# A four-layer graph network on one core: an unused buffer grows from 32 to 64 bytes per partition, and every buffer behind it moves by 32 bytes

## The reference, cut to what matters

```python
def _L0(x, adj, ...):   # 8 heads of 32, pros masked by adj; 4 hops
    q, k, v = x @ Wq.T + bq, x @ Wk.T + bk, x @ Wv.T + bv
    pros = softmax(where(adj == 0, -16384, q k^T))      # per head
    z = v
    for _ in range(4): z = 0.9 * pros @ z + 0.1 * v
    return layernorm(x + z)
def _L1(x, adj, ...):   # one head of 256
    w = softmax(where(adj == 0, -inf, (x @ Wq) (x @ Wk)^T / 16))
    return layernorm(x + (w @ (x @ Wv)) @ Wo + bo)
def _L2(x, adj, ...):   # 8 heads of 32, scaled, masked, output product with Wo
    return layernorm(x + attention(x) @ Wo + bo)
def _L3(adj, x, ...):   # 4 edge labels, mean over each label's neighbours, then a gated update
    weight = (adj == d) / (count + 1e-8)                # d = 1..4
    out = relu(concat_d(weight_d @ x) @ Wd.T + bd)
    r, z = sigmoid(out @ Wri.T + x @ Wrh.T + b), sigmoid(out @ Wzi.T + x @ Wzh.T + b)
    n = tanh(out @ Wni.T + bni + r * (x @ Wnh.T + bnh))
    return layernorm((1 - z) * n + z * x)
```

## The kernel before, in words

| buffers | bytes past a multiple of 64 |
|---|---|
| ident, ident_b, w_hi, w_lo, wo2_sb, row | 0 |
| x_in, xt_in, absent, qT0, kT0, vT0, vnat0, E0, PT0, nmax0, esum0, rsum0 | 0 |
| adj1, no_edge1, xT1, qT1, vnat1, E1, PT1 | 0 |
| absent2, qT2, kT2, vnat2 (and xT2), E2, PT2, nmax2, esum2, rsum2 | 32 |
| adj3, E3, wT, xw (and oT_hi, oT_lo, oT), xT3, rT, zT, nT, out_sb | 32 |
| y0 to y3, xn0, xn1, xT_hi0 to xT_hi3, xT_lo0 to xT_lo3 | 32 |

## Time and profile before

### The profile page before, as it was taken

The page is one execution under the profiler, slowest core; times in us unless marked ns, Lnnn a source line. Parts: engine busy times, 40 slices in busy tenths (PEclk is TensorE's granted clock), DMA queues, the critical chain, the costliest instruction groups (busy, mean ns, idle before and its releaser), DMA issues.

```text
span 1682.3 us, 44431 instructions
## 1 busy us (share of the span) xinstructions
PE 1612.9 (96%) x17552; PEld 1480.5 (88%) x17552; DVE 1131.4 (67%) x2875; ACT 1207.7 (72%) x4008; POOL 782.6 (47%) x774
## 2 busy tenths in 40 slices
PE   4788999999999999999999999999999999999985
PEld 3677999999999999999999999999999999999884
DVE  3566667677766676766667676666767666677642
ACT  4577777777777777777777777877778777777542
POOL 1345444535555454555544455454445554544521
PEclk8999999999999999999999999999999999999997
DMA  5000001110011011001101101111110111100000
GB/s 191 17 23 27 27 27 30 33 33 18 20 33 33 30 33 33 12 26 33 33 30 32 33 5 33 33 30 33 33 33 5 33 33 30 33 27 17 20 7 13
DMA packets 71135, 51.51 MB, mean 31 GB/s; under 512 B 4368, under 2 KB 69904, under 8 KB 70288
## 3 DMA queue, kind: packets, MB, share of 16 engines
q1 hardware_dynamic: 70928, 48.66, 9.4%
HBM read 40.26 MB, written 8.39 MB: 29 GB/s over the span
## 4 chain that ended last, share of the span: by engine, by line
PE 88%; ACT 4%; DVE 3%; issue 3%; POOL 1%; DMA 1%; SPq 0%; POOLq 0%; DVEq 0%; ACTq 0%
PE bank_A L375 14%; PE bank_B L375 10%; PE bank_A L601 6%; PE bank_A L592 5%; PE bank_B L592 5%; PE bank_A L419 5%; PE bank_B L419 4%; PE bank_A L405 4%; PE bank_C L413 3%; PE bank_C L375 3%; PE bank_B L387 3%; PE bank_X L375 3%; PE bank_X L387 2%; PE bank_X L527 2%; PE bank_A L393 2%
## 5 line engine op out<-in xcount | busy, mean ns | idle before, releaser
L797 POOL TENSOR_TENSOR E<-E,rsum 128x512 f32<-128x512 f32 x256 | 276.4, 1085 | 296.7 <-DVE rsum L898 180.3
L805 POOL TENSOR_TENSOR rstd<-var,minus_half 128x2 f32<-128x2 f32 x128 | 90.5, 707 | 216.8 <-DVE var L933 216.8
L375 PE MATMUL bank_A<-xT_hi,w_hi 128*128 128x256 f32 x512 | 137.9, 291 | 14.0 <-DVE xT_lo L868 11.8
L820 POOL TENSOR_TENSOR xn<-y,row 128x512 f32<-128x512 f32 x64 | 82.2, 1285 | 123.9 <-DVE y L985 122.7
L785 POOL TENSOR_SCALAR absent<-absent 128x256 int32<-128x256 int32 x64 | 57.3, 896 | 165.7 <-DMA absent<-in_adj 157.9
L375 PE MATMUL bank_A<-xT_hi,w_lo 128*128 128x256 f32 x512 | 132.4, 281 | 0.0
L891 DVE COPY_PREDICATED_SCALAR bank_A<-absent,fill 128x512 f32 x128 | 92.6, 745 | 44.6 <-PE bank_B L405 43.9
L601 PE MATMUL bank_A<-wT,xw 128*128 128x128 f32 x1024 | 119.6, 275 | 0.0
L601 PEld LDWEIGHTS bank_A<-wT,xw 128*128 128x128 f32 x1024 | 116.9, 192 | 0.0
L692 ACT ACTIVATE xT_hi<-bank_A,col 128x256 fp32r<-128x256 f32 x128 | 65.4, 561 | 70.9 <-PE bank_A L393 70.9
L375 PEld LDWEIGHTS bank_A<-xT_hi,w_hi 128*128 128x128 f32 x512 | 97.1, 190 | 16.0 <-issue 12.3
(11 more groups left out here) (197 smaller groups left out, 6024.7 us busy)
## 6 DMA issues: line engine op xcount, KB each, us to landing
xt_in<-in_xt SPq DMA_DIRECT2D x64, 128.0 KB, 3.0
absent<-in_adj SPq DMA_DIRECT2D x64, 128.0 KB, 2.8
x_in<-in_x SPq DMA_DIRECT2D x32, 256.0 KB, 3.0
adj<-in_adj SPq DMA_DIRECT2D x64, 128.0 KB, 2.8
out<-out_sb SPq DMA_DIRECT2D x32, 256.0 KB, 3.5
stage<-in_weights SPq DMA_DIRECT2D x3, 1024.0 KB, 10.8
row<-in_rows SPq DMA_DIRECT2D x1, 1152.0 KB, 10.3
stage<-in_l_weights SPq DMA_DIRECT2D x1, 1024.0 KB, 7.5
```

Of the source, the lines that this page charges most:

```text
L375: mm = nc.tensor.matmul(bank[:, oc * GN:(oc + 1) * GN], a, b, start=first and i == 0 and (last or oc == 0), stop=last and i == len(terms) ...
L797: nc.gpsimd.tensor_tensor(e, e, rs[:, part].unsqueeze(2).to_broadcast([P, SB, P]), ALU.mult).then_inc(e_sig.sem, 1)
L805: nc.gpsimd.tensor_tensor(rstd[part][:], var[part][:], minus_half[:], ALU.pow)\
L820: nc.gpsimd.tensor_tensor(to[:], y[part][:], rowc(f"gamma{part}"), ALU.mult)\
```

## The change

The unused tensor shift has 16 floats per partition instead of 8, 64 bytes instead of 32. All buffers declared behind it start 32 bytes further on; those ahead of it stay.

```diff
         minus_half = sb("minus_half", [P, G])
 
-        shift = sb("shift", [P, 8])
+        shift = sb("shift", [P, 16])
 
 
         x_in = sb("x_in", [P, G, D])
```

## The result

The changed kernel takes 1672.78 us (median of 6 runs, 1671.47 to 1673.84) against 1683.42 us before (6 runs): a ratio of 0.9937, 95% interval 0.9924 to 0.995. It is 0.6% or 10.6 us faster, where no change had been forecast. The profiled execution has a span of 1671.2 us. One run of a later kernel, the one without shift, took 1822.18 us at a mean granted clock of 0.841, against 0.984 to 0.985 in its other four, and isn't counted in that kernel's time.

What follows compares the result with a forecast made beforehand. TensorE, busy 49.24 us of each 49.24 us period, was taken as the bound. Four terms of 0 summed to no change from the profiled 1684.05 us, or 1683.3 us for the median; range 1676 to 1698 us.

Steps and rivals of the forecast that it cites:

- Points 1 and 2: Plain float32 matmuls (bounds +-0.01 us per group of four) and ACT and DVE accesses (at worst 0.5 us of ACT): cost 0.
- Landings: DMA loads into moved buffers: could land 0.2 us later or earlier, covered many times by the 49.24 us period; cost 0.
- point 4: Float32r matmuls, 192 per pair (project, natural, lab): cost taken as 0, between 5.4 us gained and 16 us lost.
- The lower bound: Natural and lab lose 3.5 ns less per matmul, 48 a period: 0.17 us a period, 5.4 us in all.
- rival D: All float32r loss comes from operands on different sides of a multiple of 64: 77 us faster, some 1606 us; chance 0.03.
- B: Weights and activations on the same side, reads meet: project up to 3.5 ns slower per matmul, +16 us, 1699 us; chance 0.30.
- C: Operand placement at 32 is what costs; natural and lab lose 3.5 ns less per matmul: -5.4 us, 1678 us; chance 0.17.

Runs made afterwards that it cites:

- xT alone: Only xT_hi, xT_lo and the small statistics behind them moved by 32 bytes, against the kernel before: 1672.01 us, ratio 0.9933.
- the map above: Small kernel of float32r matmuls alone, both operands started at all 64 pairs of 32-byte places: 113.3 to 120.0 ns a matmul by distance in the first pass.
- the first pass: Small kernel of float32r matmuls alone, 32 distances in 8-byte steps one after the other: multiples of 16 bytes 113.3 to 120.0 ns, others 119.4 to 121.7.
- the third of the small kernels: Float32r matmuls alone at distances 192 and 112, entered behind different work, and four groups of 240 at 192: two of these took 113.7 and 118.1 ns each.

## Why the prediction was wrong

The time came 3.2 us under the lower end of the range, on the side that had a chance of 0.20.

- **The bound held.** PE without a gap, 49.24 us a period, other engines with room: the gain of a period is distance between starts of matmuls, as the prediction said a change of addresses could act. Points 1 and 2 held too, to 2 ns: float32 transposes 0.59 us, kT0 and kT2 472 and 471 ns. (The 6 ns in 418 of point 2 are a row of DVE, set against ACT's 37.34 us there; of DVE's 34.67 us it is 0.5 us as well.) Landings moved by up to 0.3 us where 0.2 had been the bound (absent 3.1 us, xt_in 3.3), and in the steady part PE waits for no transfer. The landings differ from kernel to kernel without a pattern, and xT alone reached the same time with absent at 2.8 and xt_in at 3.0.
- **The step that failed is point 4,** "Nearest to the case is project itself at 117.5, since role and moving placement have been seen to matter by 1.5 ns at most. I take 0." It put a term of 144 matmuls a period at nothing. What counts is the distance between the two operands. For project with xT it went from -96 to -64, and where the term had 0, q0, k2 and q2 came down by 4.0 ns a matmul. The comparison of project with lab looks at each operand's own place, and roles swapped at 96 bytes show only -96 and +96. The kernel before did hold more. The 3.5 ns by which natural is slower than project, named in the same point as a bound and then left aside, is by the map above the difference of +96 (120.0) and -96 (117.5). And ri reads oT, which stands 32 bytes past the weights modulo 256, and ran at 116.7; the table of places modulo 64 put oT and xT in one row and hid it. No row, though, had -64, and none told which way it would go. For a rate that lost 11 ns out of 117 for no known reason, 0 was no more than a guess, and the range should have reached further on the fast side.
- **The terms.** The lower bound was -5.4 us, natural and lab alone. Natural did fall, v2 by 6.7 ns and vo1 by 1.8, but the bigger part came from project, for which the prediction had no gain short of rival D: q0, k2 and q2 fell by 4.0 ns, rh and g1 by 3.5 and 2.6. Taken from step start to step start, as medians of the steady part, k0, q0, k2, q2, g1, rh and z give some 0.25 us a period, v2 and vo1 0.10 and lab 0.07; ri and ni give back some 0.03.
- **B** came up in its reverse. Its mechanism, streams that meet more when they start alike, would fit the 120 ns at distance 0, though 96 has 120 as well, but the change set them 64 bytes apart, not 0: the side of a multiple of 64 was too coarse a reading of the addresses. At 128 bytes of shift, which does bring the distance to 0, B's sign was right (+6 us where it had priced 16).
- **C** had the sign, for a wrong reason, **D** the reason in part (the loss hangs on both placements together), but not the size: of the 11 ns that project loses to the higher clock 4 go away, and 7 stay at the best place found.
- The gap by the formula in the Trainium skill (TensorE: Matmul & The Clock Gate, Back-to-back issue gap) is 109.2 ns for 256 columns; the section calls it that of an isolated matmul and says nothing of float32r. No distance tried for float32r reached it; the best had 113.3. The Trainium skill (SBUF - State Buffer, Who interferes with whom) calls the two read ports of TensorE independent. That alone would not let one expect what was measured, that the rate depends on the distance between the two operands with no other engine at work. Whether the ports are where it comes from, no run here shows.

Open: by what the distance acts (that reads of the two streams meet in the memory is an explanation that fits, and was not observed), why v2 reached 113.3 at distance 64 when the matmuls alone stayed at 117.8, what in the entry of v0, nh, ri and ni keeps them slow, and what a place does for plain float32 products other than the transposes.

## What to carry to other kernels

Where TensorE is busy without a gap and float32r products make half of its time, the distance in SBUF between the moving and the stationary operand was worth 0.6% faster to 0.4% slower here. It changes whenever a buffer that stands between the two changes its size. Of the distance the part modulo 256 bytes is what these runs tell apart: xT moved by 288 bytes instead of 32 (the kernel with both activations moved) has q2 at 113.3 ns as well, while 64 and 192, 128 bytes apart, differ. So two versions of such a kernel that differ in any allocation should be compared at equal distances, or the layout swept in steps of 32 bytes; a gain or loss under 1% that came with a new buffer may be this alone. Read it from the starts of one step's matmuls in the steady part, where it shows to the nanosecond, and read every step, since one distance can have two paces.

## What the runs showed of the hardware that was not expected

At the granted 2.4 GHz a float32r matmul of 256 columns starts every 113.3 to about 121 ns, by the distance of its operands modulo 256 bytes: measured alone, 120.0 at 0 and at 96, 116.7 or 117.8 at 32, 117.8 at 64, 113.3 at 112 and, by entry, at 192. Off a multiple of 16 bytes it was 119 to 122 in the first pass and mostly so later. For one and the same distance, 192, there are two steady paces, 113.3 and 117.8 ns, and in the third of the small kernels what ran just ahead decided which one held for as long as the stretch lasted, 240 matmuls at most. Plain float32 transposes of y against ident (line 393 before) showed nothing of this: a median of 109 ns in all eleven kernels, though y stands in six different places against ident in them. That the label sums (out) kept 111.7 ns says little, since their two operands move together in all kernels but one.
